# Query copies, key rope and idle products at the start of a cross attention in a one-core decoder kernel

## What is computed

```python
q = jnp.einsum('bse,ef->bsf', query, Wq).reshape(nb, q_len, N_HEADS, HEAD_DIM).transpose(0, 2, 1, 3)
...
q = q * cos + _rotate_half(q) * sin
k = k * cos + _rotate_half(k) * sin
k = jnp.repeat(k, N_REP, axis=1)
v = jnp.repeat(v, N_REP, axis=1)
scale = 1.0 / jnp.sqrt(jnp.asarray(HEAD_DIM, q.dtype))
scores = jnp.einsum('bhqd,bhkd->bhqk', q, k) * scale
probs = jax.nn.softmax(scores, axis=-1)
ctx = jnp.einsum('bhqk,bhkd->bhqd', probs, v)
...
x = x + _L0_attn_ref(_layernorm(x, axis=-1), ...)
x = x + _L0_xattn_ref(_layernorm(x, axis=-1), ctx_4096, ctx_4096, itok_BxS2_0_2047, ...)
x = x + _L0_ffn_ref(_layernorm(x, axis=-1), ...)
```

## Time and profile before

| | us |
|---|---|
| median of 3 runs | 842.79 |
| lowest and highest | 842.14, 845.37 |
| the profiled execution | 841.35 |
| its span in the trace | 839.6 |
| TensorE busy in the span | 792.6 |
| VectorE, GpSimd, ScalarE busy | 629.3, 614.0, 577.2 |

### The profile page before, as it was taken

One profiled execution on the slowest core, in us unless ns is written; L12 is line 12 of the kernel. 1 busy time (PEld: TensorE's weight loads), 2 busy tenths in 40 slices (PEclk: granted clock), 3 DMA queues, 4 the chain that ended last, 5 costly groups with the idle time before them and its releaser, 6 DMA issues.

```text
span 839.6 us, 17832 instructions
## 1 busy us (share of the span) xinstructions
PE 792.6 (94%) x5624; PEld 390.4 (46%) x5624; DVE 629.3 (75%) x1189; ACT 577.2 (69%) x1056; POOL 614.0 (73%) x551
## 2 busy tenths in 40 slices
PE   5999999999999999999999999989998689999986
PEld 4464444444444444444444444444443334555442
DVE  6766776766767888677788876778868878888764
ACT  8747877777777777777777777777854455555541
POOL 7967998999978888788887888858657563333310
PEclk9999999999999999999999999999999799999999
DMA  9344355433443334344343343542221000000001
GB/s 337 135 166 142 83 169 165 141 96 84 126 103 93 90 87 104 97 101 107 95 107 92 78 109 97 134 115 54 75 74 44 1 2 2 15 14 14 15 14 39
DMA packets 52176, 75.80 MB, mean 90 GB/s; under 512 B 10256, under 2 KB 34096, under 8 KB 51616
## 3 DMA queue, kind: packets, MB, share of 16 engines
q1 hardware_dynamic: 52128, 75.23, 32.3%
HBM read 38.69 MB, written 19.40 MB: 69 GB/s over the span
## 4 chain that ended last, share of the span: by engine, by line
PE 85%; DVE 7%; ACT 3%; issue 2%; SPq 2%; DMA 1%; POOL 0%; DVEq 0%; ACTq 0%
PE PS L1495 38%; PE PS L1429 8%; PE PS L1534 7%; PE PS L1567 7%; PE PS L1568 6%; PE PS L1582 5%; PE PS L1727 2%; PE PS L1616 1%; PE PS L1607 1%; DVE xm L1277 1%; PE PS L1734 1%; PE PS L1544 1%; PE PS L1712 1%; PE PS L1693 1%; PE PS L1744 1%
## 5 line engine op out<-in xcount | busy, mean ns | idle before, releaser
L1495 PE MATMUL PS<-XTh,W 128*128 128x512 f16 x1024 | 345.9, 379 | 0.0
L653 POOL TENSOR_TENSOR Pl<-PR,Ph 128x512 f16<-128x512 f32 x254 | 286.3, 1159 | 30.9 <-ACT Ph L944 30.8
L937 ACT ACTIVATE PR<-PS 128x512 f32<-128x512 f32 x256 | 152.9, 597 | 129.5 <-PE PS L1568 122.8
L1091 DVE TENSOR_REDUCE mneg<-PS 128x4 f16<-128x512 f32 x256 | 171.5, 685 | 34.7 <-PE PS L1534 32.9
L1495 PE MATMUL PS<-XTl,W 128*128 128x512 f16 x512 | 193.6, 378 | 0.0
L1079 DVE SCALAR_TENSOR_TENSOR QS<-PS,QC 64x512 f16<-64x512 f32 x256 | 175.5, 685 | 21.0 <-ACT QC L854 16.8
L854 ACT ACTIVATE QC<-PS 64x512 f16<-64x512 f32 x256 | 150.8, 589 | 9.2 <-PE PS L1495 4.3
L1495 PEld LDWEIGHTS PS<-XTh,W 128*128 128x128 f16 x1024 | 96.5, 97 | 118.8 <-issue 25.9
L944 ACT ACTIVATE Ph<-PR 128x512 f16<-128x512 f32 x256 | 139.3, 617 | 0.0
L1534 PEld LDWEIGHTS PS<-KC,QC 112*128 112x128 f16 x1024 | 78.4, 97 | 63.4 <-DVE mneg L1091 2.8
L1567 PE MATMUL PS<-QC,KC 113*128 113x512 f16 x256 | 97.7, 382 | 3.2 <-DMA QC<-mT 1.7
(11 more groups left out here) (228 smaller groups left out, 1103.9 us busy)
## 6 DMA issues: line engine op xcount, KB each, us to landing
Wraw<-in_wqr SPq DMA_DIRECT2D x32, 512.0 KB, 5.0
QS<-QC SPq DMA_DIRECT2D x64, 256.0 KB, 3.1
head_outputs<-OS SPq DMA_DIRECT2D x256, 40.0 KB
q_content_parts<-stg SPq DMA_DIRECT2D x12, 256.0 KB, 3.0
k_content_parts<-stg SPq DMA_DIRECT2D x12, 256.0 KB, 3.1
QC<-q_content_parts SPq DMA_DIRECT2D x116, 24.0 KB
KC<-k_content_parts SPq DMA_DIRECT2D x29, 96.0 KB
xs<-in_x SPq DMA_DIRECT2D x8, 256.0 KB, 4.5
```

Of the source, the lines that this page charges most:

```text
L653: nc.gpsimd.tensor_tensor(Pl[:, 4 * j.s + b], PR[:, b], Ph[:, 4 * j.s + b], ALU.subtract).then_inc(s_pl, 1)
L937: nc.scalar.activation(PR[:, b, :], PS[:, bB[b % 2], :], ACT.Exp, scale=ATT_SCALE).then_inc(s_e, 1)
L1091: nc.vector.tensor_reduce(mneg[:, j.p, j.s, :, b], PS[:, bA[b % 2], :].rearrange("p (j k) -> p j k", j=GH), AX.X, ALU.max, negate=True).th ...
L1495: last = mm(PS[:, bQ[c], :], wt[:, j.w, k, c * P:(c + 1) * P], xt[:, k, sl], start=(i == 0), stop=(i == 3 * KT - 1))
```

## The change

ScalarE writes both high copies of a query (`query_high`), from `qr` instead of `rt`: the first at the end of a step with r = 1, the second right after the copy to `KQ` in r = 2. GpSimd keeps the low rest alone. VectorE's waits change with it: the next rope waits for its own sum, the next sum for the copies and the rest.

VectorE: the key rope's second half moves from step -2 to the end of step 1; the normalisations move (SUMS_AT; the one of the fourth block to step FIRST + 2); `norm_rows` of r = 2 stands ahead of the unit's outputs; in step -2 the maxima stand ahead of the low part. GpSimd: LOWS_AT is spread to later steps.

TensorE: `parts` takes all slices of a kind together, the low part of the data last, with a wait of its own ahead of it; gate and output product now wait for the high part first. `keep_clock` makes 17 products whose result nobody reads, in steps -2 to 2. The query product of block 1 stands behind rough scores and maxima of step -1. The output transposes of r = 2 stand behind the rough scores, and the late output pieces of steps 5 and 8 ahead of the products of r.

```diff
-        LOWS_AT = {-5: [(0, 0), (0, 1)], -3: [(0, 2), (0, 3)], 2: [(2, 0)], 3: [(1, 0)], 4: [(1, 1)], 5: [(1, 2)], 6: [(1, 3)]}
+        LOWS_AT = {-5: [(0, 0), (0, 1)], -3: [(0, 2), (0, 3)], 3: [(2, 0)], 4: [(1, 0)], 6: [(1, 1)], 7: [(1, 2)], 9: [(1, 3)]}
-        SUMS_AT = {-1: 4, 0: 5, 1: 6, 2: 7}
+        SUMS_AT = {0: 4, 2: 5, 9: 6, 13: 7}
...
-                    pool.wait_ge(s_xqp, v + 1)
...
-                    nc.gpsimd.tensor_tensor(part[0], t, t1, ALU.add).then_inc(s_qst, 1)
-                    nc.gpsimd.tensor_tensor(part[1], t, t1, ALU.add)
...
+                    pool.wait_ge(s_qst, 2 * v + 1)
                     nc.gpsimd.tensor_tensor(part[2], q, part[0], ALU.subtract).then_inc(s_xqr, 1)
...
+            def query_high(v, i):
+                act.wait_ge(s_xqa, v + 1)
+                if v == 0:
+                    act.wait_ge(s_b, 4 * NH)
+                if v >= 2:
+                    act.wait_ge(s_xt, KT * (v - 1))
+                nc.scalar.activation(qst[:, v % 2, :, XD_ * i:XD_ * (i + 1)], qr[:].rearrange("p (h d) -> p h d", d=XD_),
+                                     ACT.Copy).then_inc(s_qst, 1)
...
                 turned_out(u)
+                if r == 2 and 0 <= b + 1 < B:
+                    query_high(b + 1, 1)
...
                 x_exps(u, 1)
+                if r == 1 and 0 <= b + 1 < B:
+                    query_high(b + 1, 0)
...
-                if r == 3:
+                if r == 3 and u != -2:
                     norm_low(1, b + 2, bF[0])
...
+                if u == -2:
+                    norm_low(1, b + 2, bF[0])
+                if r == 2:
+                    norm_rows(1, b + 2)
...
                         if v >= 1:
-                            dve.wait_ge(s_xqr, v)
+                            dve.wait_ge(s_xqa, v)
+                        if v >= 2:
                             dve.wait_ge(s_kvr, 2)
...
+                        else:
+                            dve.wait_ge(s_xqr, v)
+                            dve.wait_ge(s_qst, 2 * v)
                         nc.vector.tensor_tensor(qr[:], rt[:, 0], rt[:, 1], ALU.add).then_inc(s_xqa, 1)
...
                     normalise(KT - 1, 2)
+                    normalise(KT - 1, 3)
...
-                if u == FIRST + 6:
+                if u == 1:
                     k_rope(1)
...
-                for k in range(KT):
-                    for n, (xt, wt) in enumerate([(xh, wh), (xh, wl), (xl, wh)]):
+                for n, (xt, wt) in enumerate([(xh, wh), (xh, wl), (xl, wh)]):
+                    if n == 2 and lows:
+                        pe.wait_ge(*lows)
+                    for k in range(KT):
...
+            def keep_clock(n):
+                for _ in range(n):
+                    mm(PS[:, bF[1], :], Wxh[:, 0, 0:P], Wxh[:, 0, :], start=True, stop=True)
...
+                if u in LATER and u <= 8:
+                    late_output(LATER[u])
+                if r == 0 and u != -1:
+                    query(b + 1)
...
-                        pe.wait_ge(s_oTl, v + 1)
+                        pe.wait_ge(s_oT, v + 1)
...
+                    if u == -2:
+                        pe.wait_ge(s_oe, NH)
+                        keep_clock(2)
+                    if u == 2:
+                        keep_clock(3)
                     norm_turn(1, b + 2, bF[0])
...
+                if -1 <= u <= 2:
+                    keep_clock(3)
...
                     x_rough(u + 2)
+                if r == 2:
+                    outputs_turn(b - 1)
                 if 0 <= u + 1 < NU:
                     x_max_turn(u + 1)
+                if u == -1:
+                    query(1)
```

More of the change, by code:

```diff
@@ L1745, in norm_turn, with outputs_turn, query, late_output @@
                     last.then_inc(n_tp[n], 1)
+            def keep_clock(n):
+                for _ in range(n):
+                    mm(PS[:, bF[1], :], Wxh[:, 0, 0:P], Wxh[:, 0, :], start=True, stop=True)
+            def outputs_turn(v):
+                if 0 <= v < B:
+                    pe.wait_ge(s_xon, KT * (v + 1))
+                    take(bF[0], s_oTl, v + 1)
+                    for k in range(KT):
+                        last = nc.tensor.transpose(PS[:, bF[0], k * S:(k + 1) * S], O2[:, v % 2, k * P:(k + 1) * P], ident[:])
+                    last.then_inc(s_ot, 1)
+            def query(v):
+                if 0 <= v < B:
+                    pe.wait_ge(n_tl[1], v + 1)
+                    take(bF[0], s_xqp, v + 1)
+                    pe.wait_ge(s_wxl, 1)
+                    parts(bF[0], Ah1[:, v % 2], Al1[:, v % 2], Wxh, Wxl, 0, DM).then_inc(s_xq, 1)
+            def late_output(v):
+                if v == B // 2:
+                    pe.wait_ge(s_oe, NH)
+                take(bF[1], s_x1, v + 1)
+                output(v, KT - 1)
             for u in range(FIRST, LAST):
@@ L1813, in _ @@
                         output(3, T)
[L1814 to L1819 removed]
+                if u in LATER and u > 8:
+                    late_output(LATER[u])
+                if -1 <= u <= 2:
+                    keep_clock(3)
                 if u == -2:
```

48 lines of the change are left out of this document (10 added, 38 removed).

## The result

The changed kernel takes 837.26 us (836.2 to 838.37, six runs), the kernel before, run beside it, 842.91 (842.12 to 845.64). The ratio is 0.9927, 95% interval 0.9908 to 0.9946: 5.65 us faster, where 7.95 were forecast. The profiled executions differ by 5.1 us (spans of 839.6 and 834.5).

The account below looks back on a forecast made before the run. TensorE, 94% busy, bounds the kernel; its head hangs on VectorE's order. 6.5 + 0.9 - 0.9 + 1.45 = 7.95 us off 841.35 gives 833.4, as median 834.8 us; own range 832 to 837, stated range 832.0 to 839.5.

Parts of the forecast that it names:

- The head: Units -2 to 3, start of cross attention, hanging on VectorE's order: gain 6.5 us, between 4.8 and 8.5.
- The high copy: ScalarE's high copy of a query: 0.6 us taken; above 1 us would be a sign of being wrong.
- the 3 that the prediction called wrong: Sign for the head: a key rope over 3 us would show the prediction wrong.
- Idle products and clock: Head: 17 idle products, 0.22 us each at 2.4 GHz, mostly in waits; the clock was taken to stay.
- Rival (a): The clock still falls in the head, costing about 4 us: 838.8 us; chance 0.12.
- 1.00 in every window from 640 us on: Sign in the changed profile: full granted clock from 640 us on; 0.5 anywhere there would be wrong.
- Unit 5: Late output and rough scores go ahead of output transposes; ScalarE's chain then gives half back: gain 0.9 us.
- Normalisations in steps 9 and 13: One more VectorE normalisation (1.3 us) in each, taken up by its wait at the next low part: no cost.
- Units 13 to 25: Units 13, 17, 21, 25: rough scores ahead of transposes wait for ScalarE's copy; loss 4 x 0.22 = 0.9 us.
- The tail: Last output product 1.0 us, last gate product 0.45, by high-part products going first: gain 1.45, from 0.9 to 1.8.
- step 9: Unit 8's late output moves into the 2.6 us wait of L1744: gain 0, at most 0.5 us.
- rival (b): A hop of VectorE's chain in the head is late, key rope or normalised rows: 837.2 us; chance 0.13.

Follow-up runs that it names:

- rope_back: Changed kernel with the second half of the key rope put back to the end of step -2: 838.63 us, ratio 0.9942.
- sums_lows_back: Changed kernel with the last four normalisations back in steps -1 to 2 and GpSimd's gate and base low parts in steps 2 to 6: 839.04 us, ratio 0.9940.
- x1_early: Changed kernel with VectorE's residual sums x1(4) and x1(5) moved to the head of steps 5 and 8: 833.53 us, ratio 0.9877.
- turn_first: Changed kernel with the output transposes ahead of the rough scores again in every step: 835.88 us, ratio 0.9903.

## Why the prediction was right or wrong

**The head: right in size and order, the mechanism shown in part.** 6.84 against 6.5. Rough scores 3, 4 and 5 came within 0.75 us of the forecast, VectorE's path and the key rope on it are borne out by rope_back and sums_lows_back, and what the steps are worth one by one is not. The high copy took 0.63 us against 0.6. The rope of the second half took 3.3 us, 0.5 more than the 2.8 of the sum and over the 3 that the prediction called wrong: its first instruction 0.96 and the pair behind it 1.77, where the first half took 0.69 and 0.75.
**Idle products and clock: right in the head, wrong behind it.** No window of the head is below 1.00, and without the products there are two falls. Rival (a), a fall in the head, did not come. But the prediction wanted 1.00 in every window from 640 us on and weighed falls only in the head, and the clock fell at 675 us. That the products suffice is only shown for the short waits of this order: with the rope or the tables back it fell in the head all the same.

**Unit 5: its 0.9 came, the step behind it was missed, and there the prediction failed.** The sentence that failed is "From there ScalarE's chain sets the next step as it did before". The next step is set by x1(4), the last reader of bank 7, which the output product of step 6 takes. The prediction does not follow this sum. The 0.9 that TensorE wins in unit 5 does not reach it, because its chain hangs on the output transposes, which come 0.22 us later there than the head's gain would have them: 1.16 us. And the normalised rows, which the prediction costed only in the head, stand ahead of it in step 5: 0.66. Together they make 1.82 us of wait, and behind it come 1.69 of clock in this trace; x1_early has neither. So the 0.9 was no gain. It is the largest miss, 3.5 us, and larger than the whole difference between forecast and result. The idle time is one for a bank, and the clock fell behind it in five of seven traces. The Trainium skill (TensorE: Matmul & The Clock Gate, A second HAM failure mode: psum-queue depth-cycling) tells of short idle times, while a kernel goes round its banks, that let the clock swing. The prediction weighed this for the head alone. The traces agree in that the fall came behind a wait of 1.9 us for a bank; many short waits one after the other, of which the section tells, they do not show.

**Normalisations in steps 9 and 13: wrong.** "Which its wait at the next low part takes up" holds for part of each: VectorE's wait there was shorter than 1.25 us, the rest pushed x1(6) and x1(7), and TensorE waited 0.49 and 0.43 us. 0.84 us in the trace, 0.94 given back by moving them.

**Units 13 to 25: wrong in sign, small in size.** The wait for the copy came, 0.56 us of the 0.7 forecast:

```profile
716.41 0.40 PE L1707 MATMUL PS<-KQ 48*128 48x128 f16 x8 [0.56 <-ACT KQ L1010]
716.74 0.66 PE L1772 MATMUL PS<-ident,O 128*128 128x128 f32 x4
```

The transposes behind it start at 716.74, 3.39 us earlier than at 720.13, where the stage ahead of them was 3.6 earlier: 0.2 lost, as forecast. But ScalarE's exponentials, which waited for scores that now come sooner, make it up:

```profile
717.92 0.25 ACT L995 ACTIVATE xmT<-PS 8x128 f16<-8x128 f16 x1
718.08 0.57 ACT L1002 ACTIVATE XPT<-PS 128x512 f32<-128x512 f32 x1
718.56 0.36 ACT L1058 ACTIVATE OW<-PS 128x256 f32<-128x256 f32 x1
```

These rows stand at 721.32, 721.63 and 722.23 us in the trace of before, so they come 3.40, 3.55 and 3.67 us sooner: the chain of the block, behind its copy (L1048), catches up by 0.27. The block wins 0.1 instead of losing 0.22. Over the four blocks that is +0.4 against -0.9, and step 29 adds 0.3. turn_first shows that the order of the two is nearly indifferent.

**The tail: right.** 1.27 against 1.45, and 1.42 lost when it is undone, 0.87 of it at the output product and 0.55 at the gate product (forecast 1.0 and 0.45).

**The sum.** Forecast 7.95. Step 6 took 3.5, the normalisations 0.84 and step 9 0.17; the blocks gave 1.5 more than forecast, head and unit 5 0.4 more, the tail 0.2 less: 7.95 - 3.5 - 0.84 - 0.17 + 1.5 + 0.4 - 0.2 = 5.1, the gain of the trace; the medians give 5.65. The measured 837.26 lies within the stated range up to 839.5, but just above 832 to 837, the forecast's own. That it is off by no more than 2.5 us is in part luck: losses of 4.5 us that the prediction did not have meet 1.9 us that it did not have either. The time of rival (b), 837.2, is that measured, but by coincidence: its price counts the 0.7 us of the rope again that are already in the sum, the rope cost 0.5 more, not 1.7, and the normalised rows took 0.54 us in the head.

## What to carry to other kernels

When a step is moved ahead on an engine, list everything that stood behind its new place in every iteration, not only in the one that the move is for, and ask of each whether it is the last reader of a bank. Where a path gets shorter, ask whether the last reader of the bank that it takes next gets earlier by as much; if not, what was won turns into a wait. The parts of a retimed head cannot be priced one by one: here three of four lost 1.6 to 5.2 us when they were undone, and the largest brought 0.2 alone; in that trace the clock fell earlier and VectorE waited out what it had been spared. Before a copy is given to a faster engine, ask whether its input could not be finished first.

## What the runs showed of the hardware

- The same wait ahead of the same product (1.89 us in six traces, 2.11 in one) was followed by 1.2 GHz in five traces and not in two, one of them that of 2.11; the fall costs 1.7 us each time. Without the wait it did not come there in four traces. Shortening a wait can therefore pay more than the wait, by a part that one trace cannot give.
- Twelve kernels that differ little up to 639 us reach rough scores 0 anywhere from 642.0 to 645.4 us. Lengths inside one trace repeat to 0.02 us between kernels, where medians of four to ten runs leave 2 us open.
- GpSimd's plain copy of 128x512 from f32 to f16, with gaps in the result, takes 0.6 us. Its sum of two tiles of that size took 1.76 us, while VectorE summed the same tiles beside it, and 1.27 when made again right behind.
